# The first stages of a graph-attention kernel: norm by groups of four tiles, products on GpSimd, sums over neighbours in two column tiles, later waits

## The reference

```python
seq = (layernorm(x) @ W_seq).reshape(N, H, DH)      # N 2048, H 16, DH 32
score1 = einsum('nhd,d->hn', seq, a1); score2 = einsum('nhd,d->hn', seq, a2)
scores = leaky_relu(score1[:, :, None] + score2[:, None, :], 0.2)
scores = scores + (1.0 - adj)[None, :, :] * -65500.0
hidden = einsum('hij,jhd->ihd', softmax(scores, axis=-1), seq)
```

## Time and profile before

| | us |
|---|---|
| median of 3 runs | 2346.68 (2344.52 to 2347.96) |
| the profiled execution, as timed | 2353.32 |
| its span, first to last instruction | 2351.6 |
| stage a | 0 to 102.80 |
| stage f, with the wait at its end | 103.38 to 114.93 |
| stage m | from 114.93 |

### The profile page before, as it was taken

How to read it: one execution, slowest core, us unless ns; L and a number is a source line. 1 busy time by engine, 2 the same in 40 slices (tenths; PEclk the granted TensorE clock), 3 DMA queues, 4 the chain that set the end, 5 groups by cost and what they waited for, 6 DMA issues and landing times. The chain is left out here.

```text
span 2351.6 us, 43031 instructions
## 1 busy us (share of the span) xinstructions
PE 2117.2 (90%) x18260; PEld 1238.6 (53%) x18260; DVE 1557.5 (66%) x2507; ACT 1090.1 (46%) x1071; POOL 552.0 (23%) x413
## 2 busy tenths in 40 slices
PE   6799999999996899969999998999992599999997
PEld 3444444444443344434444444444461488888886
DVE  7768888888885766747777778776336544444442
ACT  5667888888882233313344444444431222222221
POOL 0000000000001112333454555545521222222211
PEclk9899999999998999958999999999976699999999
DMA  7421211212114111353113031011030444444431
GB/s 253 142 62 42 72 52 62 75 39 76 49 47 156 64 50 72 136 124 76 29 28 82 19 80 29 23 37 46 23 135 36 152 117 117 117 117 113 113 66 23
DMA packets 81711, 185.27 MB, mean 79 GB/s; under 512 B 8785, under 2 KB 18001, under 8 KB 75985
## 3 DMA queue, kind: packets, MB, share of 16 engines
q1 hardware_dynamic: 72560, 161.56, 21.0%
q0 software_dynamic: 8960, 20.98, 4.8%
HBM read 137.81 MB, written 40.37 MB: 76 GB/s over the span
## 5 line engine op out<-in xcount | busy, mean ns | idle before, releaser
L450 ACT ACTIVATE m_step<-m_ub,gat_bias 128x2048 bf16<-128x2048 f32 x256 | 494.3, 1994 | 119.7 <-DVE m_mask L527 106.2
L1266 DVE TENSOR_REDUCE t_rm<-t_m 128x1 f32<-128x512 f32 (+3 forms) x640 | 373.2, 606 | 167.9 <-PE t_m L1374 98.2
L1196 ACT ACTIVATE t_E<-t_s 128x1024 f32<-128x1024 f32 (+3 forms) x320 | 277.7, 896 | 426.9 <-PE t_s L1391 224.8
L527 DVE TENSOR_TENSOR m_mask<-m_step,gat_adjT 128x2048 bf16<-128x2048 bf16 x256 | 306.8, 1222 | 84.8 <-ACT m_step L450 72.8
L1143 POOL TENSOR_TENSOR t_total<-t_E 128x1024 f32<-128x1024 f32 (+2 forms) x160 | 308.1, 1938 | 209.5 <-PE t_d L1418 204.5
L567 PE MATMUL m_bd<-m_mask,m_S 128*32 128x512 bf16 x3072 | 211.9, 380 | 8.1 <-DVE m_mask L527 7.8
L567 PE MATMUL m_bd<-gat_adjT,m_S 128*32 128x512 bf16 x3072 | 211.8, 380 | 4.9 <-PE m_dn L567 4.9
L567 PE MATMUL m_bd<-m_mask,m_neg 128*32 128x512 bf16 x3072 | 211.4, 380 | 0.0
L1374 PE MATMUL t_m<-tq_K,tq_Q 96*128 96x512 f32 (+2 forms) x320 | 145.3, 482 | 34.5 <-DVE t_rm L1266 16.5
L1756 POOL DMA_INDIRECT out<-e_ye,e_token x40 | 80.9, 2024 | 350.4 <-DVE e_ye L1858 341.6
L1922 PE MATMUL e_h<-e_xTh,e_w1h 128*128 128x320 f32 x512 | 159.6, 312 | 3.5 <-PE e_y L1941 2.1
(11 more groups left out here) (306 smaller groups left out, 3689.9 us busy)
## 6 DMA issues: line engine op xcount, KB each, us to landing
a_adj<-in_adj SPq DMA_DIRECT2D x16, 1024.0 KB, 4.9
m_ub<-scratch_uac SPq DMA_DIRECT2D x16, 1024.0 KB, 4.7
e_w1r<-in_L_ffn_w SPq DMA_DIRECT2D x8, 2048.0 KB
e_w2r<-in_L_ffn_w SPq DMA_DIRECT2D x8, 2048.0 KB, 8.8
tq_Q<-scratch_parts SPq DMA_DIRECT2D x48, 256.0 KB, 4.8
m_scale<-scratch_uac SPq DMA_DIRECT2D x32, 256.0 KB
scratch_parts<-o_hi SPq DMA_DIRECT2D x32, 256.0 KB, 2.1
scratch_parts<-o_lo SPq DMA_DIRECT2D x32, 256.0 KB, 2.4
```

The costliest lines, as they stand in the source:

```text
L450: act.activation(step[n % RELUS][:, :], ub[h % 2][:, :], ACT.Relu, bias=bias[:, j, h:h + 1], scale=BIG).then_inc(step_ready, 1)
L527: dve.tensor_tensor(mask[n % MASKS][:, :], step[n % RELUS][:, :], adjT[:, j, :], ALU.min).then_inc(mask_ready, 1)
L1196: act.activation(E[n % 3][:, two, off:BANK], ps_s[:, two, off:BANK], ACT.Exp, scale=SCALE).then_inc(exp_done[z], 1)
L1266: dve.tensor_reduce(rm[:, h, t, ch:ch + 1], ps_m[i % 2][:, 0:w], AX, ALU.max).then_inc(entry_read, 1)
```

## The change

Stage a: x is normalised four tiles at a time, the second to fourth group inside the tile loop; the transfers are reordered; the transposed x gets three buffers in place of one for all tiles; the products by the attention vectors of tiles 0 to 14 move to GpSimd, and the reductions of tile t follow the copy of tile t + 1. Stage f: the rows of u are copied and sent first, the others later, and the wait for landing moves to the user in stage m. Stage m: the near products get 64 columns (16 of them are thrown away) and two chunks side by side, accumulated in one bank at partitions 0 and 64; the picking sums move behind step 2 of head 0; waits for GpSimd's constants are split by user; `rows` shares its memory with `scale`.

```diff
 # stage a, SP
+                load_x(0)
+                sp.dma_start(W[:, :, :], w_seq.rearrange("(k p) n -> p k n", p=P)).then_inc(w_in, 16)
+                load_adj(0)
+                for a, dst in ((a1, arow[0]), (a2, arow[1])):
+                    sp.dma_start(dst[:, :], a.partition_broadcast(P)).then_inc(a_in, 16)
+                load_x(1)
+                load_adj(1)
+                load_x(2)
+                load_x(3)
+                for t in range(2, T):
+                    load_adj(t)
 # stage a, GpSimd
+                pool.memset(keep["Dp64"][:, T * SPLITS * H:], 0.0).then_inc(consts, 1)
+                pool.wait_ge(a_in, 32)
+                for t in range(T - 1):
+                    pool.wait_ge(seq_ready, t + 1)
+                    if t >= 1:
+                        pool.wait_ge(dots_done, 2 * t)
+                    sv = seq[:, t, :].rearrange("p (h d) -> p h d", h=H)
+                    for n in range(2):
+                        pool.tensor_tensor(prod[n][:, :, :], sv, arow[n][:, None, :].to_broadcast([P, H, DH]),
+                                           ALU.mult).then_inc(prod_done, 1)
 # stage a, ACT
+                def root(c):
+                    act.wait_ge(ve_ready, c + 1)
+                    act.activation(sd[:, 4 * c:4 * c + 4], ve[:, 4 * c:4 * c + 4], ACT.Sqrt).then_inc(sd_ready, 1)
...
+                root(0)
                 for t in range(T):
                     act.wait_ge(xT_full, t + 1)
+                    if t >= 3:
+                        act.wait_ge(seq_full, t - 2)
...
                     cast(t)
+                    if t < 3:
+                        root(t + 1)
                     if t >= 1:
                         store(t - 1)
 # stage a, DVE
+                def normalise(c):
+                    four = range(4 * c, 4 * c + 4)
+                    cut = slice(4 * c, 4 * c + 4)
+                    dve.wait_ge(x_in[c], 16)
+                    for t in four:
+                        dve.bn_stats(stats[:, t, :], X[:, t, :]).then_inc(stats_done, 1)
+                    dve.wait_ge(stats_done, 4 * c + 4)
+                    for t in four:
+                        last = dve.bn_aggr(mv[:, t, :], stats[:, t, :])
+                    lk(last)
+                    dve.tensor_scalar(ve[:, cut], mv[:, cut, 1], LN_EPS, None, ALU.add).then_inc(ve_ready, 1)
+                    dve.wait_ge(sd_ready, c + 1)
+                    root_of_inverse(dve, lk, rstd[:, cut], sd[:, cut], ve[:, cut])
+                    for t in four:
+                        dve.tensor_scalar(X[:, t, :], X[:, t, :], mv[:, t, 0:1], rstd[:, t:t + 1],
+                                          ALU.subtract, ALU.mult).then_inc(xn_ready, 1)
+
+                def dots(t):
+                    for n, s in enumerate((s1, s2)):
+                        dve.wait_ge(prod_done, 2 * t + n + 1)
+                        dve.tensor_reduce(s[:, t, :], prod[n][:, :, :], AX, ALU.add).then_inc(dots_done, 1)
+
+                normalise(0)
                 for t in range(T):
+                    if t < 3:
+                        normalise(t + 1)
                     dve.wait_ge(adj_cast, t + 1)
...
                     dve.tensor_copy(seq[:, t, :], ps_s[t % 2][:, :]).then_inc(seq_ready, 1)
-                    dve.wait_ge(seq_ready, t + 1)
-                    sv = seq[:, t, :].rearrange("p (h d) -> p h d", h=H)
-                    for n in range(2):
-                        dve.tensor_tensor(prod[n][:, :, :], sv, arow[n][:, None, :].to_broadcast([P, H, DH]),
-                                          ALU.mult).then_inc(prod_done, 1)
...
+                    if t >= 1:
+                        dots(t - 1)
+
+                dve.wait_ge(dots_done, 2 * T - 2)
+                dve.wait_ge(seq_ready, T)
+                dve.wait_ge(a_in, 32)
+                for n in range(2):
+                    dve.tensor_tensor(prod[n][:, :, :], seq[:, T - 1, :].rearrange("p (h d) -> p h d", h=H),
+                                      arow[n][:, None, :].to_broadcast([P, H, DH]), ALU.mult).then_inc(prod_done, 1)
+                dots(T - 1)
 # stage f
+                dve.wait_ge(turned, 1)
+                dve.tensor_copy(rows[:, 0:2, :], p0[:, 0:2 * P].rearrange("p (n q) -> p n q", q=P)).then_inc(rows_ready, 1)
                 lk(dve.tensor_scalar(bias[:, :, :], sv[:, :, :], BIG, None, ALU.mult))
...
+                sp.wait_ge(rows_ready, 1)
+                sp.dma_start(view[:, 0:2, :], rows[:, 0:2, :]).then_inc(rows_out, 16)
                 sp.wait_ge(rows_ready, 2)
...
-                sp.wait_ge(rows_out, 16)
+                sp.dma_start(view[:, 2:6, :], rows[:, 2:6, :]).then_inc(rest_out, 16)
 # stage m
+                sp.wait_ge(u_out, 16)
                 load_u(0)
+                sp.wait_ge(ac_out, 16)
                 sp.dma_start(crow[0:H, :], uac_dram[2, :, :]).then_inc(crow_in, 16)
...
-                dve.wait_ge(setup, 10)
+                dve.wait_ge(setup, COUNTS)          # 3: dscale and den are set
                 for part in range(3):
                     prepare(0, part)
+                for b in range(2):
+                    near_evict(b)
                 for h in range(H):
                     for j in range(T):
-                        if h == 0 and j == 2:
-                            near_evict(0)
-                            near_evict(1)
-                            for c in range(2):
-                                near_scale(c)
-                                near_evict(c + 2)
-                        if h == 0 and j == 4:
-                            near_scale(2)
-                            near_scale(3)
+                        if h == 0 and j in (4, 6):
+                            near_scale(j - 4)
+                            near_scale(j - 3)
...
-                def near_product(c):
+                def near_product(b):
                     for j in range(T):
-                        mm = pe.matmul(gbank[c][0:GR, :], Dp[:, j, :, :].rearrange("p s h -> p (s h)"),
-                                       adjT[:, j, c * BANK:(c + 1) * BANK], start=(j == 0), stop=(j == T - 1))
+                        for c in range(2):
+                            mm = pe.matmul(gbank[b][GR * c:GR * (c + 1), :], Dp64[:, j * SPLITS * H:j * SPLITS * H + GR],
+                                           adjT[:, j, (2 * b + c) * BANK:(2 * b + c + 1) * BANK],
+                                           start=(j == 0), stop=(j == T - 1))
                     mm.then_inc(near_full, 1)
...
-                pe.wait_ge(setup, 10)
-                for c in range(4):
-                    near_product(c)
-                for c in range(4):
-                    near_total(c)
+                for b in range(2):
+                    near_product(b)
...
                         mm.then_inc(mask_free, 1)
+                        if h == 0 and j == 2:
+                            for c in range(4):
+                                near_total(c)
```

More of the change, by code:

```diff
@@ L80, in stage_sequence @@
         X = keep["V"]
-        xT = st.sb("xT", [P, KD, N])
+        xT = [st.sb(f"xT{i}", [P, KD, P]) for i in range(3)]
         W = st.sb("w", [P, KD, D])
@@ L111, in _, with load_x, load_adj @@
                 xv = x.rearrange("(t p) d -> p t d", p=P)
-                for c in range(4):
+                def load_x(c):
                     sp.dma_start(X[:, 4 * c:4 * c + 4, :], xv[:, 4 * c:4 * c + 4, :]).then_inc(x_in[c], 16)
[L114 to L117, removed]
+                def load_adj(t):
                     if t >= 2:
@@ L381, in _ @@
                     pool.memset(den[r][:, :, :], 0.0).then_inc(setup, 1)
+                pool.memset(pick3[:, :, :], 0.0).then_inc(setup, 1)
+                pool.memset(pick[:, :, :], 1.0).then_inc(setup, 1)
                 pool.wait_ge(setup, 5)
+                for c in range(2):
+                    for s in range(SPLITS):
+                        pool.affine_select(out=pick3[:, c, :], in_=pick3[:, c, :], compare_op=ALU.not_equal, fill=1.0,
+                                           base=-GR * c - H * s, pattern=[[-1, H]], channel_multiplier=1).then_inc(setup, 1)
+                        pool.wait_ge(setup, 6 + SPLITS * c + s)
                 pool.affine_select(out=pick[:, :, :], in_=pick[:, :, :], compare_op=ALU.is_ge, fill=0.0, base=0,
                                    pattern=[[-TILE, 4], [0, TILE]], channel_multiplier=1).then_inc(setup, 1)
-                for s in range(SPLITS):
-                    pool.affine_select(out=pick3[:, :], in_=pick3[:, :], compare_op=ALU.not_equal, fill=1.0,
-                                       base=-H * s, pattern=[[-1, H]], channel_multiplier=1).then_inc(setup, 1)
-                    pool.wait_ge(setup, 7 + s)
+                pool.wait_ge(setup, 12)
                 pool.affine_select(out=pick[:, :, :], in_=pick[:, :, :], compare_op=ALU.is_ge, fill=0.0, base=5,
@@ L407, in load_scales @@
                     else:
[L408 removed]
```

(21 more changed lines are left out.)

77 lines of the change are left out of this document (30 added, 47 removed).

## The result

| | before | after |
|---|---|---|
| median of 15 runs each | 2344.62 (2341.41 to 2352.68) | 2339.95 (2334.12 to 2348.76) |
| ratio, 95% | | 0.9975 (0.9963 to 0.9987) |
| the profiled execution, its span | 2353.32, 2351.6 | 2337.5, 2335.8 |

The account below looks back on a forecast made before the run. PE, busy 90% of the span, and whatever delays its start were taken as the bound. Terms +5.7 + 0 - 2.4 - 12.8 = -9.5 took the median from 2346.7 to 2337.2 us; own range 2332 to 2342, 8 in 10 2331 to 2349.

Parts of the forecast that it names:

- The beginning: Stage a: early PE start eaten by DVE, then slow passes and late reductions; +5.7 us, bounds +2 and +8.
- The second chunk lands at 14.9: Start of stage a: second chunk of x lands where the fourth did, 14.5, plus 0.4 for two small rows.
- DVE's chain of 24.9: Stage a ramp: DVE's work from the second chunk until tile 2 can be turned, 24.9 us, ending at 39.8.
- Slow passes cost 2.3: Stage a after tile 2: PE's clock falls after idling, slow passes cost +2.3 us; bounds 0 and +4.
- Reductions at the end 1.3: End of stage a: tile 14's reductions stand between tile 15's copy and its products, +1.27 us.
- GpSimd's products: Stage a tiles: GpSimd keeps up and one DVE wait is hidden; cost 0, at worst the price of DVE held twice.
- second rival: Stage a tiles: GpSimd holds DVE at both lines 179 and 180, ends slower, 2355; chance 0.20, half of it slower.
- Factors stage and border: Stage f to m: SP's wait for the rows' landing goes, engines enter the mask stage 2.4 us earlier: -2.4.
- fourth rival: Head 0 of stage m waits for u, landing 3 us later; gain 6.5, 2340; chance only within a joint 0.68.
- Start of head 0: Start of stage m: earlier, paired near products bring step 1 forward, less four sums; -12.8 us, bounds -13.5 and -4.5.
- four sums for 1.7: Head 0 of stage m: four picking sums added to PE, 4 x 0.43 = 1.7 us at full clock.
- third rival: Stage a ramp: PE keeps its clock, x lands early, stage a only +2; 2333.5; chance only within a joint 0.68.

Follow-up runs that it names:

- e6: Kernel after with the broadcasts of the two attention vectors moved behind the third chunk of x; 2338.53 us, one run.
- e7: Kernel after with 64 idle transposes on PE ahead of the turn of tile 2; 2336.18 us, one run.
- e2: Kernel before with only the new stage a, stages f and m as before; ratio to before 1.0021 (1.0009 to 1.0033).
- e5: Kernel after with the products by the attention vectors back on DVE, behind the copy in each tile; 2336.74 us, one run.
- e1: Kernel after with stage a as before, keeping only the three transposed-x buffers and 16 zero columns; ratio to before 0.9950 (0.9933 to 0.9968).
- e9: Kernel after with old stage a, 12 of 16 normalisations inside its tile loop, two picking sums inside step 0 of head 0; ratio to before 0.9933.
- e3: Kernel after with the second chunk of x right behind the first in the transfer queue; 2331.15 us, one run.
- e4: Kernel after with the near products of one bank made one chunk after the other instead of in alternating pairs; 2347.77 us, one run.

## Why the prediction was right, and where it was off

The sign and the place of each gain came out; of the sum −9.5 the mark shows −7.1, and the timed runs −5.9 (−8.7 to −3.0). That the time itself, 2337.2 forecast and 2339.95 measured, comes nearer than the gain is luck: the 15 runs of before have a median 2.1 below the 3 runs from which I started. By the steps:

**1. The beginning: +5.7 forecast, +5.8 measured. The path is the one forecast, but three terms were off and cancelled, so the close hit is luck.**
- *The second chunk lands at 14.9*: 17.08. This is the step that failed. Its price for the two small rows, 0.4, stood on no row, and e6 shows 2.6.
- *DVE's chain of 24.9*: 24.0 (17.08 to 41.08). Right: DVE, not PE, sets the ramp.
- *Slow passes cost 2.3*: 1.3 in this execution, by e7. Here only the transposes were slow (0.83 and 0.45 more), and the clock was back for the products (3.67 against 3.60). In e2, with the same instructions, most products were slow too and the spell cost 2.9. So 2.3 lies within what the executions show; that the one profiled came out cheap is chance.
- *Reductions at the end 1.3*: the timeline of after has just that ahead of the last products:

```profile
104.81 1.27 DVE L211 TENSOR_REDUCE s_s<-a_prod 128x16 f32<-128x512 f32 x2
106.12 1.29 DVE L230 TENSOR_TENSOR a_prod<-gat_seq,a_row 128x512 f32<-128x512 f32 x2
107.33 1.27 DVE L211 TENSOR_REDUCE s_s<-a_prod 128x16 f32<-128x512 f32 x2
```

The measured terms are +3.35 (41.08 − 37.73), +1.27 and +1.27, together 5.9.

**2. GpSimd's products: 0 forecast, 0 in the steady tiles.** The hold exists, once in a tile at most and in only five of the tiles, and the pace stays 4.78. The second rival's condition (line 179 held too) is not met: line 218, which stands for it after, is over before a product starts. In the ramp the move is worth some 3.3, by e5; my sum had it there, in the 24.9.

**3. Factors stage and border: −2.4 forecast, −2.0 measured** (3.16 to 1.16). In e1, e5 and e9, where GpSimd has no products in stage a, the border takes 0.77 to 0.78 (e1: from 111.81 to 112.59), which is the −2.4 forecast; in the six other kernels with the new border it takes 1.16, and e2, with the old border, has 3.53 where before has 3.16. So 0.4 goes with the products on GpSimd, a term that my sum did not have; why they lengthen a border that comes 14 us later stays open. u is not late: ACT's step starts at 126.41, S + 7.7, as forecast. The fourth rival (waiting for u) falls.

**4. Start of head 0: −12.8 forecast, −10.9 measured.** Near products 8.8 for 8.6, step 1 at S + 12.5 for S + 12.4. What was mis-sized is the last term, four sums for 1.7: they are eight passes and take 3.4 (135.56 on, 0.86 each); 14.4 won at step 1 less 3.4 is the 10.9 of the mark, within 0.1. The row has four passes, which are two sums, in 1.89. I put that down to a clock at half for part of them, and counted one pass of 0.43 to a sum. The clock was not slow there; the window of before (granted clock third from the end):

```profile
133.43:135.32 1.89, 1.89 (x5) 0.29 (x4) 0.76 (x2) 0.00 (x0) 0.00 (x0) 1.00 0.00 0
```

Before taking a duration per item from a merged row, count how many instructions an item has, and look up the clock instead of supposing it.

The third rival (PE keeps its clock and stage a costs 2) did not come, but e6 shows how near it was: with the small rows sent later PE keeps its clock from tile 2 on (4.78 to tile 3) and stage a costs 2.2.

## What to carry to other kernels

An early start of the bound engine is worth only what its feeder can follow with: here PE began 9.3 sooner and was 3.4 later at the third tile, since DVE's work was the same and in more pieces. Tell the parts of a change apart at landmarks inside the trace when the timed runs can't resolve them; here two of three stages were worth 12.4 us and the third cost 5.3. Before a landmark is trusted to 1 us, read it in more than one execution of the same instructions. Where a transfer is late, look at what stands ahead of it in the queue, and not by its bytes alone: here 32 KB cost as much as 1 MB.

## What the hardware showed that I had not expected

- Two transfers of 16 KB, spread over 128 partitions in rows of 128 bytes, cost a queue of 1 MB transfers 2.6 us; the rate in that stretch was 115 GB/s instead of 406, with the DMA engines busy for 0.34 of it, and the stretch moved with the rows (e6, e3).
- Matmuls of different column tiles overlap even when they do not alternate in the program. In e4 16 passes to one half of the columns are followed by 16 to the other; if only neighbours in program order could overlap, the three borders would save 3 x 0.21 = 0.6. The fast passes at 0.21 would be 11.3 (53 of them), and took 9.3: 2.0 less. So passes must have been taken out of program order. The windows of e4 fit: near a border eight passes lie in half a us, elsewhere four. No view shows the passes one by one, so the order itself is worked out, not seen. The Trainium skill ("TensorE: Matmul & The Clock Gate", Part 3: Packing small matmuls — row/col tiling) has matmuls start and end strictly in program order; by that these passes would have saved 0.6 at most, and the measurement stands against it.
- How long PE's clock stays at half (0.50, 1.2 GHz) at the start of stage m differs between executions of the same instructions: for 3.1 us of the near products in e5 and 5.8 in e1, and they took 8.61 and 9.97, the ends of the range in the runs with pairs. The spell after tile 2 scatters likewise (1.3 in after, 2.9 in e2). That is 1.4 and 1.6 us of scatter in a landmark, as much as the smallest effects looked for here.
